# The end of product five's wide columns, and the loads of its residual rows, in a kernel of six matrix products on one core

## What is computed

```python
x = _layernorm(x + _L0_gnn_ref(x, ..., adj, adj, ...), axis=-1)   # adj @ (scale * (adj @ (x @ w))) + bias
x = _layernorm(x + _L1_gnn_ref(..., x, adj, ...), axis=-1)        # relu(inv_deg * A' @ x @ W.T + b)
x = _layernorm(x + _L2_gnn_ref(x, adj, ...), axis=-1)
x = _layernorm(x + _L3_gnn_ref(x, adj, ...), axis=-1)             # relu([x, adj @ x] @ W.T + b)

def _L2_gnn_ref(x, A, W1, b1, W2, b2, sigma, k):                  # k = 4, sigma = 1
    z = leaky_relu(_lap_mul(A, x) @ W1 + b1)
    d2 = sq[:, None] + sq[None, :] - 2.0 * (z @ z.T)
    S = exp(-sqrt(max(d2, 0) + 1e-10) / (2.0 * sigma))
    S = where(rank of S in its row < k, S, 0.0)
    return _lap_mul(S + A, x) @ W2 + b2
```

## Time and profile before

| | us |
|---|---|
| median of 3 runs | 1469.2 |
| lowest and highest of them | 1463.95, 1472.29 |
| the profiled execution | 1465.6 |
| its span (first to last instruction) | 1463.7 |
| PE busy in the span | 1393.7 (95%) |
| DVE, ACT, POOL busy | 836.0, 451.0, 246.9 |

### The profile page before, as it was taken

One profiled execution on the slowest core, in us unless ns is written; L12 is line 12 of the kernel. 1 busy time (PEld: TensorE's weight loads), 2 busy tenths in 40 slices (PEclk: granted clock), 3 DMA queues, 4 the chain that ended last, 5 costly groups with the idle time before them and its releaser, 6 DMA issues.

```text
span 1463.7 us, 20350 instructions
## 1 busy us (share of the span) xinstructions
PE 1393.7 (95%) x7300; PEld 737.9 (50%) x7300; DVE 836.0 (57%) x1311; ACT 451.0 (31%) x979; POOL 246.9 (17%) x358
## 2 busy tenths in 40 slices
PE   6999999999999799999999987999999889999997
PEld 4776676666444354444544532444444344444454
DVE  6877766665224423323322269999999356555044
ACT  4776665665100000000000045666666200000011
POOL 2111110111100100000000000111111277774000
PEclk9999999999999999999999999999999989999999
DMA  9999998897998979788778520004443799999962
GB/s 311 400 383 389 365 331 300 325 318 266 359 382 331 379 308 346 306 316 328 298 292 310 227 72 1 15 17 137 134 130 115 242 370 401 380 386 394 352 234 71
DMA packets 112814, 403.26 MB, mean 276 GB/s; under 512 B 10368, under 2 KB 28384, under 8 KB 91232
## 3 DMA queue, kind: packets, MB, share of 16 engines
q1 hardware_dynamic: 72672, 314.33, 57.8%
q0 software_dynamic: 20576, 77.07, 14.0%
q10 hardware_dynamic: 19488, 10.80, 2.4%
HBM read 337.67 MB, written 64.49 MB: 275 GB/s over the span
## 4 chain that ended last, share of the span: by engine, by line
PE 70%; DVE 10%; DMA 10%; issue 7%; ACT 2%; POOL 0%; ACTq 0%; SPq 0%; DVEq 0%; POOLq 0%
PE acc L1137 10%; PE acc L1138 9%; PE acc L1139 9%; PE pt L1201 4%; DMA at_scratch<-region 3%; PE pt L1277 3%; PE pt L1278 3%; PE pt L1279 3%; DVE hT L1021 3%; PE pt L1137 3%; PE pt L1139 3%; PE pt L1138 3%; DMA region<-in_adj 3%; PE acc L1186 2%; PE acc L1182 2%
## 5 line engine op out<-in xcount | busy, mean ns | idle before, releaser
L1137 PE MATMUL acc<-region,yop 128*128 128x512 f16 x681 | 259.6, 381 | 16.6 <-DMA region<-at_scratch 16.6
L1201 PE MATMUL pt<-ident,region 128*128 128x128 f32 x1024 | 243.1, 277 | 18.8 <-DMA region<-in_adj 9.6
L1138 PE MATMUL acc<-region,yop 128*128 128x512 f16 x681 | 259.5, 381 | 0.0
L1139 PE MATMUL acc<-region,yop 128*128 128x512 f16 x681 | 259.5, 381 | 0.0
L969 DVE SCALAR_TENSOR_TENSOR region<-pt,region 128x512 f16<-128x512 f32 x200 | 135.3, 686 | 76.9 <-ACT region L631 76.4
L1201 PEld LDWEIGHTS pt<-ident,region 128*128 128x128 f32 x1024 | 145.9, 143 | 61.2 <-issue 16.1
L677 ACT ACTIVATE region<-pt 128x512 f32<-128x512 f32 x256 | 132.8, 602 | 109.4 <-PE pt L1284 95.8
L631 ACT ACTIVATE region<-pt 128x512 f16<-128x512 f32 x200 | 117.8, 596 | 108.6 <-PE pt L1201 94.0
L1021 DVE MAX8 hT<-region 128x8 f32<-128x4096 f32 x32 | 141.2, 4411 | 2.4 <-ACT region L677 2.4
L1137 PEld LDWEIGHTS acc<-region,yop 128*128 128x128 f16 x681 | 66.7, 98 | 98.7 <-issue 14.6
L598 ACT ACTIVATE std<-mv,eps_ln 128x4 f32<-128x4 f32 x32 | 9.5, 297 | 334.5 <-DVE mv L803 334.5
(11 more groups left out here) (235 smaller groups left out, 2157.8 us busy)
## 6 DMA issues: line engine op xcount, KB each, us to landing
region<-at_scratch SPq DMA_DIRECT2D x166, 1280.0 KB, 7.8
region<-in_adj SPq DMA_DIRECT2D x64, 1024.0 KB, 8.9
at_scratch<-region POOLq DMA_DIRECT2D x40, 768.0 KB, 7.0
at_scratch<-region POOLq DMA_DIRECT2D x40, 512.0 KB, 7.6
region<-at_scratch SPq DMA_DIRECT2D x76, 256.0 KB, 2.7
x_scratch<-xout ACTq DMA_DIRECT2D x16, 256.0 KB, 12.3
gath_all<-x_scratch POOLq DMA_DIRECT2D x12, 256.0 KB, 4.1
xin<-at_scratch SPq DMA_DIRECT2D x12, 256.0 KB, 2.8
```

The source lines that it names most:

```text
L1137: nc.tensor.matmul(into, y[:, 0, kt, :], high, start=(kt == first_tile), stop=False)
L1138: nc.tensor.matmul(into, y[:, 0, kt, :], low, start=False, stop=False)
L1139: return nc.tensor.matmul(into, y[:, 1, kt, :], high, start=False, stop=(kt == last_tile))
L1201: ins = nc.tensor.transpose(pt[kt % 4][:, t * P:(t + 1) * P], nat[u % 4][:, t, (kt % TPC) * P:(kt % TPC + 1) * P], ident[:, :])
```

## The change

Three things change.

- Columns 24, 25 and 26 are still done from tiles. The last five wide columns, 27 to 31, are exactly the last unit of a chunk, and are now taken from whole units, chunk by chunk: `LATE` gets four entries at its head, (4, 0..3, last unit), and PE does 15 matmuls for each. `LATE_AT` goes. SP loads the first of them as soon as row 30 of the search is done, ahead of the tiles of column 26; the second and third behind these tiles when the search is over; the fourth when all tiles are used. The three early units of the narrow part are no longer loaded ahead.
- The residual rows come in four pieces (`RES_PIECES`), each of four transfers of 128 KB, issued by ACT: two pieces before ACT's copies of chunks 0 to 3, two behind these.
- DVE waits for a piece, and adds its bias, ahead of the first of its two chunks.

```diff
-WIDE_REST = [24, 25, 26, 27, 28, 29, 30, 31]
-LATE_AT = {29: 0, 30: 1, 31: 2}
+WIDE_REST = [24, 25, 26]
+LAST_TILE_COLUMN = 26
...
-        LATE = ([(4, c, u) for c in range(WIDE, NCH) for u in range(UPC)]
+        LATE = ([(4, c, UPC - 1) for c in range(WIDE)]
+                + [(4, c, u) for c in range(WIDE, NCH) for u in range(UPC)]
...
-            for kt in range(KEPT, KT):
+            for kt in range(KEPT, LAST_TILE_COLUMN + 1):
                 u, k = divmod(kt - KEPT, UNIT)
+                if kt == LAST_TILE_COLUMN:
+                    sp.wait_ge(near_used, KT - 1)
+                    load_late(0)
...
-                if kt in LATE_AT:
-                    sp.wait_ge(near_used, KT - 1 if LATE_AT[kt] == 0 else KT)
-                    load_late(LATE_AT[kt])
-
-
-            sp.wait_ge(acc_full, nth(ALL, 4, WIDE - 1))
+            sp.wait_ge(near_used, KT)
+            load_late(1)
+            load_late(2)
+            sp.wait_ge(tile_used, (LAST_TILE_COLUMN + 1 - KEPT) * WIDE)
+            load_late(3)
...
-            pool.wait_ge(near_full, KT * NCH)
-            x2_rows = x_dram[2].rearrange("(c t p) f -> p t c f", p=P, t=TPC)
-            for t in range(TPC):
-                pool.dma_start(res_rows(t // 2, 0, NCH)[:, :, t % 2, :], x2_rows[:, t, :, :]).then_inc(res_loaded, 16)
...
+            def load_residual(q):
+                x2_rows = x_dram[2].rearrange("(c t p) f -> p t c f", p=P, t=TPC)[:, :, q * PIECE:(q + 1) * PIECE, :]
+                for t in range(TPC):
+                    act.dma_start(res_rows(t // 2, q * PIECE, PIECE)[:, :, t % 2, :], x2_rows[:, t, :, :]
+                                  ).then_inc(res_loaded[q], 16)
+
             act.wait_ge(xT_ready, nth(XTS, 4, NCH - 1))
+            act.wait_ge(near_full, KT * NCH)
+            load_residual(0)
+            load_residual(1)
             for c in range(SUMS_AHEAD):
                 act_epilogue(act, 4, c, None)
+            load_residual(2)
+            load_residual(3)
...
             def residual(c):
+                if c % PIECE == 0:
+                    residual_bias(c // PIECE)
...
                 wide_products(kt)
                 if kt == WIDE_REST[1]:
                     pe_project_x2(pe, NCH - 1)
+            pe.wait_ge(yop_ready, nth(YOP, "y", NCH - 1))
+            for c in range(WIDE):
+                chunk_columns(4, c, range(LAST_TILE_COLUMN + 1, KT)).then_inc(acc_full, 1)
```

More of the change, by code:

```diff
@@ L50 @@
 X3_BUFFERS = 3
+RES_PIECES = 4
 WIDE_AT = {i: i - 8 for i in range(8, 32)}
@@ L75, in gnn_kernel @@
     NAT_UNITS = KT // TPC
+    PIECE = NCH // RES_PIECES
     XT_PART = KT // X_PARTS
@@ L248, in gnn_kernel @@
         late_used = sem("late_used")
-        res_loaded = sem("res_loaded")
+        res_loaded = [sem(f"res_loaded{q}") for q in range(RES_PIECES)]
         gath_used, x3_used = sem("gath_used"), sem("x3_used")
@@ L435, in _ @@
                 sp.wait_ge(y_stored[b], 16 * NCH // 2)
-            for k in range(len(LATE_AT), len(LATE)):
+            for k in range(4, len(LATE)):
                 load_late(k)
@@ L813, in layernorm, with residual_bias @@
                 dve.wait_ge(xout_ready, nth(XIN, p, c))
-            def residual_bias():
-                dve.wait_ge(res_loaded, 16 * TPC)
+            def residual_bias(q):
+                dve.wait_ge(res_loaded[q], 16 * TPC)
                 for half in range(2):
-                    held = res_rows(half, 0, NCH).rearrange("p c t f -> p (c t) f")
-                    step(nc.vector.tensor_tensor(held, held, bias[4][:, :].unsqueeze(1).to_broadcast([P, 2 * NCH, D]), ALU.add))
+                    held = res_rows(half, q * PIECE, PIECE).rearrange("p c t f -> p (c t) f")
+                    step(nc.vector.tensor_tensor(held, held, bias[4][:, :].unsqueeze(1).to_broadcast([P, 2 * PIECE, D]), ALU.add))
             def residual(c):
+                if c % PIECE == 0:
+                    residual_bias(c // PIECE)
                 dve.wait_ge(nat_full, nth(ALL, 4, c))
@@ L1042, in _ @@
                 for t in range(TPC + 1):
-                    if (c, t) == (0, 1):
-                        residual_bias()
                     for ahead in RESIDUAL_AT.get((c, t), []):
@@ L1340, in wide_products @@
                     last = products(4, late_acc(4, c), kt, hi, lo)
-                    if kt == KT - 1:
-                        last.then_inc(acc_full, 1)
-                    elif kt >= KEPT:
+                    if kt >= KEPT:
                         last.then_inc(tile_used, 1)
```

## The result

| | kernel before | changed kernel |
|---|---|---|
| median of 20 runs each, us | 1469.55 | 1473.55 |
| lowest and highest | 1463.95, 1474.23 | 1468.61, 1477.55 |
| span of the profiled execution | 1463.7 | 1470.5 |

The ratio is 1.0034, with a 95% interval from 1.0023 to 1.0044: the changed kernel is 4.0 us slower, which is inside the 0.5% that the prediction called no change. It had said 1475.7, +6.5 us.

A forecast was written before the change was run, and what follows sets the result against it. PE was taken to set the time: 19 us gained at the wide part's end, then two stops on residual rows, netting +5.7 to +7.4, middle +6.5. 1469.2 + 6.5 = 1475.7 us; range 1462 to 1487.

The forecast's parts named there:

- the 19 us: End of the wide columns: with whole units PE finishes at 1167.9 instead of 1186.92, 19 us on offer.
- What bounds the kernel now, and the first edit: PE sets the time, losing some at the wide columns' end; four units of 12.95 us end there at 1167.9.
- Behind the wide part they have as much to do as before: DMA engines in the narrow part: unchanged work; ring buffers return after 13 us, landings take 9.9, at most 11.8.
- The gathers, put at 1159: POOL, rid of four issues and a 10.70 us stand, begins the gathers near 1159, not at 1170.23.
- The DMA ceiling of 4.5 to 6.4 us: At the end PE can be ahead by only 4.5 to 6.4 us, not 19, even with no further wait.
- Packets in turn, 38 rows a microsecond: Engines alternate ACT's 512 B rows with SP's 10240 B runs, one packet each; ACT's queue moves 38 rows/us.
- First stop: Before chunk 1's projection: piece 0 lands about 1187, so PE stands some 15 us from 1174.6.
- I am wrong if the first piece lands before 1170: Sign on the first residual piece's landing time: landing before 1170 would mean rows do not hold up PE.
- Second stop: Before chunk 5's projection: chunk 0's store waits behind residual rows; PE stands 9 us, projection begins at 1237.6.
- No third stop: Product 5: a possible further PE stop from chunk 4's late split, priced at 0.
- 2.1 us of half clock: After the second stop, PE at half clock for 4.8 us loses 2.1 us on ten matmuls.
- B: Rival on residual loads: rows do not hold up PE, DMA engines bound it; -4.5 to -7.4 us, 1463; chance 0.17.

The follow-up runs named there:

- e5: Changed kernel with the 16 residual-row loads issued by SP instead of ACT: 1459.55 us, ratio 0.9936 to the kernel before.
- e8: Kernel before, tile loads kept, with the residual rows in four pieces issued by SP: 1463.00 us, ratio 0.9956 to the kernel before.
- e6: Changed kernel with the narrow part's first unit loaded into the slot already free: 1475.46 us, ratio 1.0051 to the kernel before.
- e9: Changed kernel with each residual load cut to 128 rows, result incomplete: 1459.08 us, ratio 0.9923 to the kernel before.

## Why the prediction was right, and where its steps were not

The predicted sum was +6.5 us; the medians gave +4.0 and D5 gave +4.8. The form was right: the units bring the 19 us, residual rows issued by ACT take them back and a little more, in two stops, each followed by half the clock. Step by step:

- *What bounds the kernel now, and the first edit.* Right. The wide part ended at 1169.9, with the 1.7 us of chance taken off at 1168.2; predicted 1167.9. No tile waits behind the search's end, and the four units came in time.
- *"Behind the wide part they have as much to do as before", narrowest spare 1.2 to 3.1 us.* Failed at one place. I did not ask what SP waits for before the first unit of the narrow part, now that none is loaded ahead: the store of `y`, 8.4 us. This gave 4.16 us and half the clock behind them. The gathers, put at 1159, began at 1165.84 for the same reason.
- *The DMA ceiling of 4.5 to 6.4 us.* Too low. e5 stands 8.3 us ahead of the kernel before with the same bytes. The ceiling was worked out with the rows' packets where they were; e8 shows that the place of the rows alone is worth 4.3 to 6.0 us.
- *Packets in turn, 38 rows a microsecond.* Right as a rate: 73 beside 76 packets here, 37 a microsecond in e6. It did not hold throughout (822 beside 467 packets from 1192 to 1206 us). So the trace speaks for one row a packet in ACT's queue, as rows 6 and 7 did, and against the 9 to 17 descriptors that the Trainium skill calls typical (DMA: Bandwidth & Descriptors, Queues, rings and completion order); its rule that the engines take the queues in turn a packet at a time holds.
- *First stop: piece 0 at 1187, 15 us.* Missed, by the prediction's own sign too ("I am wrong if the first piece lands before 1170"). Piece 0 came at 1167.8, since SP's queue ran empty while SP waited for the store of `y`. I had given that case its price (1024 packets in 2 us) but not looked for where it would occur. What PE waited for before the projection of chunk 1 was 2.21 us of `residual(0)`, which was late by the gathers, not by the rows. e6 shows the landing, 3 us from the figure, when SP does not wait; a stop of 15 us by it was seen in no run.
- *Second stop: before the projection of chunk 5, 9 us, by the store of chunk 0.* It was 12.6 us, and place and cause were wrong. It came one projection earlier, because ACT stood 15.5 us inside two issues. The prediction let ACT issue both pieces in 3 us, "at 1196 to 1199", by the 0.39 us of a single issue; they took 18.56. The rows of before had the sign: POOL's fourth load waited 10.70 us for "issue", and I took it as POOL's matter. Where the second eight issues do not stand (e6 and e9), the store's stop is there, before chunk 5.
- *No third stop.* Right: no PE wait behind the projection of chunk 5.

So the total came out near partly by luck: 24 us of standing predicted and 19.3 measured, split otherwise and for other causes, and 2.1 us of half clock predicted, 3.6 measured. The projection of chunk 5, put at 1237.6, began at 1238.68, of which 1.7 are chance: the right moment by the wrong way. What was sound is the balance of 19 us brought against rows that hold up PE for about as long. Of the rivals, B (rows do not hold up PE, -4.5 to -7.4) is near what the kernel becomes when SP issues them (-8.3 and -7.8).

## What to carry to other kernels

An issue instruction is not free: ask how many rows are on their way in the issuing engine's queue when it comes, and what that engine has to compute next. Small-row loads belong on an engine that computes nothing and at a point where it waits anyway; here that turned a change that cost 4 us into one that gives 8. When loads ahead are taken away, look up every wait that stood in front of the next ones.

## What the runs showed of the hardware

- An engine that issues loads of 256 rows of 512 B stood in the sixth (5.56 us in the changed kernel's first group, 4.57 in the second), and in the eighth for up to 15.5 us (e6). With 128 rows in each load none of eight stood (e9). POOL stood as well, before its fourth load of 1024 rows (10.70 and 16.81 us), and SP in e5 and e8 for up to 6.5 and 5.6 us, with nothing to compute behind it. An estimate from these: ACT stopped with some 1,300 to 1,500 rows on their way, five or six loads of 256. It is no fixed bound: e6's second group, eight loads, did not stand at all.
- The same rows moved at 37 a microsecond beside a full queue of 10240 B runs (e6) and at 416 when that queue was nearly empty and POOL's idle: a factor of eleven, by what the other queues held.
